# Step sizes of two state-space layers: the bias moved into the product, the correction shared with GpSimd, two PSUM pairs in turn

## What is computed

```python
def _L0_attn_ref(x, A_log, D, W_xproj, W_dt, b_dt):
    x_proj = jnp.einsum('bld,ed->ble', x, W_xproj)
    dtp = x_proj[..., :DT_RANK]                       # 64 columns; 16 of B and 16 of C follow
    dt = jax.nn.softplus(jnp.einsum('blr,dr->bld', dtp, W_dt) + b_dt)
    ...
    # h = exp(dt * A) * h + dt * B * x ;  y = sum over 16 states of h * C ;  y + D * x

def _L1_attn_ref(x, W_delta, W_dt, b_dt, W_B, W_C, A_log, D):
    delta = _softplus_thresh(x @ W_delta @ W_dt + b_dt)     # 128 columns
    ...

x = x + _layernorm(_L0_attn_ref(_layernorm(x), ...))
x = x + _layernorm(_L0_ffn_ref(_layernorm(x), ...))
x = x + _layernorm(_L1_attn_ref(_layernorm(x), ...))
x = x + _layernorm(_L1_ffn_ref(_layernorm(x), ...))
```

## Time and profile before

| | us |
|---|---|
| runs of the kernel before | 656.8, 658.79, 659.71 (median 658.79) |
| span of the profiled execution, first to last instruction | 657.3 |
| granted TensorE clock, mean | 0.977 of full |
| PE / DVE / ACT / POOL busy | 602.7 / 530.2 / 513.7 / 429.1 |
| first stage, to the first scan step | 49.35 |
| scan steps of layer 0 | 49.35 to 206.6 |
| sign product and middle stage | to 282.08 |
| scan steps of layer 1 | 282.08 to 437.6 |
| mixture of experts | to 657.3 |

### The profile page before, as it was taken

How to read it: one execution, slowest core, us unless ns; L and a number is a source line. 1 busy time by engine, 2 the same in 40 slices (tenths; PEclk the granted TensorE clock), 3 DMA queues, 4 the chain that set the end, 5 groups by cost and what they waited for, 6 DMA issues and landing times.

```text
span 657.3 us, 12812 instructions
## 1 busy us (share of the span) xinstructions
PE 602.7 (92%) x4540; PEld 501.7 (76%) x4543; DVE 530.2 (81%) x899; ACT 513.7 (78%) x1182; POOL 429.1 (65%) x261
## 2 busy tenths in 40 slices
PE   5898999999996569799999999999999999999992
PEld 3388999999996434599999999989677555555662
DVE  6798999999998789989999999987863566555374
ACT  2999999999995798899999999967544665444335
POOL 0037999999999302479999999995004277777403
PEclk8979999999999699999999999999999999999997
DMA  7022333333331000044544454438112133333173
GB/s 198 6 67 65 112 112 105 108 109 114 103 110 32 2 0 7 19 147 134 180 128 153 145 159 155 147 91 274 43 64 65 33 97 97 97 99 96 56 265 128
DMA packets 41596, 67.78 MB, mean 103 GB/s; under 512 B 6688, under 2 KB 20928, under 8 KB 41536
## 3 DMA queue, kind: packets, MB, share of 16 engines
q1 hardware_dynamic: 37696, 56.50, 27.5%
q0 software_dynamic: 3840, 10.49, 5.1%
HBM read 57.28 MB, written 9.70 MB: 102 GB/s over the span
## 4 chain that ended last, share of the span: by engine, by line
PE 57%; DVE 14%; ACT 13%; POOL 8%; DMA 4%; issue 3%; DVEq 1%; SPq 0%; ACTq 0%; POOLq 0%
PE both L1383 16%; PE bank L1412 12%; POOL arena L1184 7%; PE both L1476 7%; PE both L1385 5%; PE both L1463 4%; PE bank L1483 4%; DMA arena<-w 2%; ACT rings L1045 2%; PE bank L1404 2%; DVE arena L658 2%; DVE st L443 1%; PE bank L1584 1%; ACT rings L923 1%; ACT tok_a L996 1%
## 5 line engine op out<-in xcount | busy, mean ns | idle before, releaser
L1184 POOL TENSOR_TENSOR arena<-arena,rings 128x1024 f32<-128x1024 f32 x126 | 296.8, 2375 | 17.5 <-DVE arena L658 13.4
L1383 PE MATMUL both<-rings,tok_a 128*128 128x128 f32 x1280 | 183.3, 277 | 3.6 <-DVE arena L658 2.2
L1383 PEld LDWEIGHTS both<-rings,tok_a 128*128 128x128 f32 x1280 | 164.6, 193 | 5.1 <-issue 2.9
L658 DVE TENSOR_TENSOR_SCAN arena<-rings,both 128x1024 f32<-128x1024 f32 x64 | 145.3, 2279 | 12.3 <-PE both L1385 4.5
L658 DVE TENSOR_TENSOR_SCAN arena<-late,both 128x1024 f32<-128x1024 f32 x62 | 140.7, 2278 | 7.1 <-PE both L1385 1.8
L1412 PE MATMUL bank<-ident,arena 128*128 128x128 f32 x1024 | 133.0, 273 | 2.8 <-POOL arena L1184 1.4
L1412 PEld LDWEIGHTS bank<-ident,arena 128*128 128x128 f32 x1024 | 115.7, 141 | 4.2 <-POOL arena L1184 1.9
L1045 ACT ACTIVATE rings<-ident,b_tok 128x128 f32<-128x128 f32 x320 | 106.6, 394 | 0.3
L1045 ACT ACTIVATE rings<-tok_a,b_tok 128x256 f32<-128x256 f32 x192 | 89.7, 500 | 0.0
L1385 PE MATMUL both<-ident,rings 128*128 128x128 f32 x384 | 84.0, 273 | 0.0
L1199 POOL TENSOR_TENSOR arena<-arena,feat_a 128x512 f32<-128x512 f32 x8 | 19.4, 2425 | 86.2 <-DVE arena L554 86.2
(11 more groups left out here) (233 smaller groups left out, 1045.9 us busy)
## 6 DMA issues: line engine op xcount, KB each, us to landing
rings<-c_rows SPq DMA_DIRECT2D x128, 256.0 KB, 3.2
w_sb<-w SPq DMA_DIRECT2D x18, 352.0 KB, 4.2
arena<-w SPq DMA_DIRECT2D x2, 2048.0 KB, 13.2
residual<-x SPq DMA_DIRECT2D x4, 512.0 KB, 5.8
x_rows<-tok_a SPq DMA_DIRECT2D x4, 512.0 KB, 2.6
tok_a<-y_tok SPq DMA_DIRECT2D x4, 512.0 KB, 6.3
w_sb<-y_tok SPq DMA_DIRECT2D x4, 512.0 KB, 7.0
out<-residual SPq DMA_DIRECT2D x8, 256.0 KB, 2.6
```

The lines of the kernel that those rows point to most:

```text
L658: dve.tensor_tensor_scan(h_s, decay_s.rearrange("p h t -> p (h t)"), both[s % B_RING][:, :], 0.0, ALU.mult, ALU.add).then_inc(h_ready, 1)
L1184: pool.tensor_tensor(h_both, h_both, c_row, ALU.mult).then_inc(hc_ready, 1)
L1383: pe.matmul(o, tok_a[:, c, h * P:(h + 1) * P], v_ring[:, s % V_RING, j, 0:P], start=True, stop=True)
```

## The change

It does four things, in both layers:

- **The bias goes into the product.** In layer 0 the tile that holds the projected columns gets a row of ones (row 96; rows 64 to 95 hold B and C), and W_dt gets zero rows and the bias as row 96: one product with 97 rows. In layer 1 all 128 rows are in use, so a second product is added per half (L1306 of the changed kernel): a 128-row block whose first row is the bias, times a 128x512 tile of ones, accumulated in the same bank. The loads of the two bias columns go, one load of a bias block for layer 1 is new.
- **ACT and DVE work is cut.** `Relu` (ACT) and `relu` (DVE) go. `Abs` has no bias. `Exp` and `Ln` take both halves in one instruction of 1024 columns; `Ln` takes 1 + e through its bias and waits for `Exp` only. DVE `near` makes (e + 1) - 1 for both halves in one instruction, and subtracts it from e for half 0; POOL does that for half 1 (`lost`). DVE `dt` then reads the product from PSUM: max(v, 0) + the correction, one instruction per half, and adds the logarithm.
- **PSUM.** `pre` alternates between two pairs of banks, and is released by DVE's `dt` (pre_free) in place of ACT.
- **Order.** The lists are rewritten around this.

```diff
+PRE_ROWS = (64 + 2 * 16 + 1, 128)
...
+        one_row = early[:, 0:SEQ]
+        b_row = early[:, SEQ:SEQ + D]
...
+        pre_pair = [[pairs[1], pairs[2]], [pairs[1], pairs[3]]]
...
-        u_bank = [bank[4:6], bank[6:8]]
+        u_bank = [bank[6:8], bank[4:6]]
...
-            ("x_stat", 0), ("x_norm", 0), ("x_stat", 1), ("x_norm", 1), ("x_stat", 2), ("x_norm", 2), ("x_stat", 3), ("err", 0),
-            ("x_norm", 3), ("ffn", 0), ("err", 1), ("dt", 0), ("err", 2), ("dt", 1), ("b_cols", 1), ("err", 3), ("dt", 2), ("dt", 3)]
+            ("x_stat", 0), ("x_norm", 0), ("x_stat", 1), ("x_norm", 1), ("x_stat", 2), ("x_norm", 2), ("x_stat", 3), ("near", 0),
+            ("x_norm", 3), ("dt", 0), ("ffn", 0), ("near", 1), ("dt", 1), ("near", 2), ("dt", 2), ("b_cols", 1), ("near", 3), ("dt", 3)]
...
-        pool_middle = [("y_add", q) for q in range(Q)] + [("dt", q) for q in range(Q)]
+        pool_first = [("lost", 0), ("dt", 0), ("lost", 1), ("dt", 1), ("lost", 2), ("dt", 2), ("lost", 3), ("dt", 3)]
+        pool_middle = [("y_add", q) for q in range(Q)] + pool_first
...
-                elif name == "err":
-
-                    for h in range(H):
-                        i = k * H + h + 1
-                        dve.wait_ge(exp_ready, i)
-                        dve.tensor_scalar(w_buf[:, h, t], uT[:, h, t], 1.0, None, ALU.add).then_inc(w_ready, 1)
...
+                elif name == "near":
+
+                    if k == Q:
+                        keep()
+                    dve.wait_ge(exp_ready, k + 1)
+                    dve.tensor_scalar(dtT[:, :, t], uT[:, :, t], 1.0, -1.0, ALU.add, ALU.add).then_inc(near_ready, 1)
+                    dve.wait_ge(near_ready, k + 1)
+                    dve.tensor_tensor(dtT[:, 0, t], uT[:, 0, t], dtT[:, 0, t], ALU.subtract).then_inc(lost0_ready, 1)
...
+                        dve.wait_ge(lost_ready if h else lost0_ready, k + 1)
+                        dve.scalar_tensor_tensor(dtT[:, h, t], pre_half(l, q, h), 0.0, dtT[:, h, t], ALU.max, ALU.add)\
+                           .then_inc(head_ready if h == 0 else pre_free, 1)
...
-                        if l == 0:
-                            act.activation(dtT[:, h, t], bank[2 + h][:, :], ACT.Relu, bias=bdt_sb[l][:, h:h + 1])
...
+                    act.wait_ge(exp_ready, k + 1)
+                    act.activation(w_buf[:, :, t], uT[:, :, t], ACT.Ln, bias=ones[:, 0:1]).then_inc(ln_ready, 1)
...
+                    pool.wait_ge(near_ready, k + 1)
+                    pool.tensor_tensor(dtT[:, H - 1, t], uT[:, H - 1, t], dtT[:, H - 1, t], ALU.subtract).then_inc(lost_ready, 1)
...
+                    elif q >= 2:
+                        pe.wait_ge(pre_free, k - 1)
+                    if l:
+                        for h in range(H):
+                            pe.matmul(pre_half(l, q, h), b_row[:, h * P:(h + 1) * P], one_row, start=True, stop=False)
+                    pe.wait_ge(proj_copied, k + 1)
...
+                        if l == 0 and q == 0:
+                            pe.wait_ge(fwT_copied, 1)
+                        stay_busy(turns_behind_u[q], bank[1])
```

More of the change, by code:

```diff
@@ L185, in sandwich_kernel @@
         bank = [both[i // H][:, i % H * SEQ:(i % H + 1) * SEQ] for i in range(H * B_RING)]
-        bank += [ctx.enter_context(nc.psum_tensor(f"bank{i}", [P, 512], F32)) for i in range(H * B_RING, 8)]
+        pairs = both + [ctx.enter_context(nc.psum_tensor(f"pair{i}", [P, H * SEQ], F32)) for i in range(B_RING, 4)]
+        bank += [pairs[i // H][:, i % H * SEQ:(i % H + 1) * SEQ] for i in range(H * B_RING, 8)]
+        pre_pair = [[pairs[1], pairs[2]], [pairs[1], pairs[3]]]
         ysum = bank[4:6]
@@ L274, in sandwich_kernel @@
             ("x_norm", 0), ("r_add", 1), ("r_stat", 2), ("x_stat", 1), ("r_add", 2), ("x_norm", 1), ("r_stat", 3), ("x_stat", 2),
-            ("r_add", 3), ("x_stat", 3), ("x_norm", 2), ("relu", 0), ("x_norm", 3), ("err", 0), ("relu", 1), ("dt", 0), ("err", 1),
-            ("relu", 2), ("dt", 1), ("err", 2), ("relu", 3), ("b_cols", 1), ("dt", 2), ("err", 3), ("dt", 3)]
+            ("r_add", 3), ("x_stat", 3), ("x_norm", 2), ("near", 0), ("x_norm", 3), ("dt", 0), ("near", 1), ("dt", 1), ("near", 2),
+            ("b_cols", 1), ("dt", 2), ("near", 3), ("dt", 3)]
         scalar_middle = [
@@ L574, in stage @@
                     scale(name, q)
-                elif name == "relu":
-                    if k == Q:
-                        keep()
-                    for h in range(H):
-                        dve.wait_ge(pre_used, k * H + h + 1)
-                        dve.tensor_scalar(dtT[:, h, t], bank[2 + h][:, :], bdt_sb[l][:, h:h + 1], 0.0, ALU.add, ALU.max)\
-                           .then_inc(relu_ready, 1)
                 elif name == "r_stat":
@@ L1199, in stage @@
                     pool.tensor_tensor(uT[:, H - 1, t], dtT[:, H - 1, t], feat_a[:, H - 1, t], ALU.mult).then_inc(u_ready, 1)
+            pool.memset(dtpT[PRE_ROWS[0] - 1:PRE_ROWS[0], :], 1.0).then_inc(ones_ready, 1)
+            pool.wait_ge(ones_ready, 1)
+            pool.memset(one_row, 1.0).then_inc(ones_ready, 1)
             for decay in abar_pair:
                 pool.memset(decay[:, :, H - 1, 0:1], 0.0).then_inc(edge_ready, 1)
-            for q in range(Q):
-                stage("dt", q, 0)
+            for name, q in pool_first:
+                stage(name, q, 0)
             product(0)
```

86 lines of the change are left out of this document (37 added, 49 removed).

## The result

| | before | changed |
|---|---|---|
| median of the runs, us | 659.25 (656.8 to 662.13) | 667.01 (664.12 to 669.29) |
| ratio of changed to before | | 1.0108 [1.0074, 1.0142] |
| span of the profiled execution | 657.3 | 664.7 |
| last scan step of layer 0 | 204.25 | 205.83 |
| last scan step of layer 1 | 435.29 | 441.70 |

The change costs 1.1%. (The ratio and its 95% interval are the record's; it is not exactly the quotient of the two medians. The median before is 659.25 with a fourth run, 658.79 with the three that the prediction had.) Of the 7.4 us between the two profiled spans 1.58 arise in layer 0, 4.83 between the two last steps, 1.0 in the experts. The prediction had 0.1, 4.3 and 0.

The account below looks back on a forecast made before the run. PE and DVE were both full in layer 1's middle stage, PE's bias products deciding: span 657.3 + 4.3 (layer 1) + 0.1 (layer 0) = 661.7, plus 1.5 for the runs' median: 663.2 us; range 658.8 to 667.2.

Parts of the forecast that it names:

- Bias pair 1.72, period 8.0, no gap: Layer 1's middle stage on PE: two bias products per quarter cost 1.72 us, period 8.0, last `pre` ends 6.6 later.
- Faster: Rival: DVE sets the middle stage and PE only fills up behind it; total -3 to -5 us, 654 to 656; chance 0.11.
- Nothing to measure: Rival: DVE and POOL follow closely, layer 0 gains 1.2 us, scan catches up; +0.5 to +2.5, 659.3 to 661.3; chance 0.19.
- Much slower: Rival: POOL shut out in both layers, 1.5 to 3 us more in layer 0, 1.5 in layer 1; 666 to 669; chance 0.13.
- PE sets the middle stage: Layer 1, before its scan: PE's added products decide, 6.6 us on PE; last `Exp` at 273.5 against 268.89.
- The chain of dt of quarters 2 and 3 through POOL: Layer 1 entry: DVE waits for POOL until 281.1, dt ready 283.2, so `decays 1` start at 283.5, not ACT's 282.8.
- An entry that ACT sets: Layer 1 scan: 156.1 us from `decays 1` to the last step, as in layer 0, against 157.1 before; +4.3 us in all.
- First stage: Layer 0 up to its scan: ACT's savings of 5 us stay hidden; `decays 1` +0.1 us, from -1.2 to +1.5.
- Reason (a): Layer 0: DVE and POOL work per quarter is 6.2 us against 6.1 before, so no gain.
- Reason (b): Layer 0: the scaling of a_sb, which `decays 0` wait for, moves one quarter later, behind `dt` of quarter 2, to 42.3.
- Exclusion of DVE and POOL: DVE and POOL shut each other out; of a POOL product's 1.65 us about 0.5 is waiting, 1.13 its own.
- The experts "untouched": After layer 1's scan: the experts keep their time and only start later by the same amount; no added cost.

Follow-up runs that it names:

- no_bias1: Changed kernel without the eight bias products of layer 1, whose bias is left out of the result; 658.20 us, ratio to the kernel before 0.9956.
- before_bias: Kernel before, with two bias products (zeros) per quarter of layer 1 added ahead of `pre`; 666.81 us, ratio to the kernel before 1.0108.
- before_load97: Kernel before, with layer 0's W_dt loaded as 97 rows in place of 64; 660.49 us, ratio to the kernel before 1.0006.
- before_again: Kernel before, unaltered, run once more for a second trace; 658.93 us (one run).
- load112: Changed kernel with layer 0's W_dt loaded as 112 rows in place of 97; 665.86 us, ratio to the kernel before 1.0073.
- lost_dve: Changed kernel with the correction of both halves on DVE and none on POOL; 664.34 us, ratio to the kernel before 1.0038.
- mends_lost_dve: Changed kernel with W_dt as 112 rows, layer 1's bias moved from PE to ACT and DVE, both corrections on DVE; 657.09 us, ratio 0.9955.
- early_scale: As mends_lost_dve, but the scaling of a_sb stands behind `near` of quarter 2, not behind its `dt`; 656.23 us, ratio to the kernel before 0.9932.

## Why the prediction was right, and where it was not

- **The total.** The median, 667.01, lies inside the range of 658.8 to 667.2 with 0.2 us to spare, above the forecast's own 661 to 665.5, and 3.8 above 663.2. Direction and main term were right; that the total still fell inside the range is in part luck. As a ratio the forecast was 1.0067 (663.2 / 658.79), and the measurements are 1.0108 [1.0074, 1.0142] and, in twelve more runs, 1.0089 [1.0061, 1.0118]. Of the 3.0 us by which the profiled span exceeds the forecast's 661.7, 1.5 are layer 0, 0.5 the middle stage and 1.0 the tail.
- **Bias pair 1.72, period 8.0, no gap.** All three as the rows show (1.72, 8.01). This term decided: no_bias1 and before_bias put it at 6.8 and 6.15 us, where the prediction had 6.6 on PE.
- **The rivals.** *Faster* (DVE sets the middle stage) falls with before_bias. *Nothing to measure* needed 1.2 us of gain in layer 0, which lost instead. *Much slower* has the measured total in its 666 to 669, but not its mechanism: POOL's product of 4.7 us doesn't occur in the changed kernel, whose longest POOL product there takes 2.25 and whose longest subtraction 1.79.
- **"PE sets the middle stage".** Right for the changed kernel. The last `Exp` came at 276.33; less the 1.58 of layer 0 that is 274.75, where 273.5 was forecast. The 1.25 are the low clock ahead of the first `pre`, a term the sum did not have. In the profiled kernel before, that stretch was at full clock by chance; the other level costs that kernel 0.72 at `decays 1`. The reading of the earlier trace rows, PE without a gap, didn't tell that half a microsecond of it was free.
- **The chain of dt of quarters 2 and 3 through POOL (281.1, 283.2, `decays 1` at 283.5).** Wrong as a mechanism: that dependence doesn't exist. `decays 1` were set by ACT, 9.23 after the last `Exp`. The prediction had ACT's own value, 282.8, and put 0.7 on top (0.3 of it, from 283.2 to 283.5, without a reason); less 1.58 the decays came at 283.98, which is 282.8 + 1.25 within 0.1. An error of 0.7 and a missing 1.25 partly cancel, so +4.3 against a measured 4.83 looks better than its working.
- **An entry that ACT sets takes 156.1 to the last step.** 156.14 here. The figure is right, the reason isn't: from `decays 1` to the last step it is 156.12 to 156.14 in layer 0 of all fourteen profiles and in layer 1 of twelve. The 157.1 of the kernel before (and 157.10 in before_load97) isn't another kind of entry, but the low clock at its first scan steps. So the 1.0 us that the prediction subtracted is a clock level in one profile and not a gain of the change. Against before_again, without that loss, "between" is 5.07 longer in the changed kernel.
- **First stage +0.1.** Measured 1.58, just past the bound of 1.5 that the prediction had named for being wrong, and itself a sum of three things. The late x is 2.06 (load112, at like clock). The rest of the change is 0.87: load112 against before_again, both with full clock between 12 and 16 us and 0.50 between 36 and 40 (203.77 against 202.90). And 1.35 goes off, because the first profile of the kernel before had lost that much against before_again, with its clock at 0.57 between 12 and 16. The 0.87 goes with PE: the fourth `pre` starts 0.3 earlier in load112 (32.29 against 32.59), but behind the wait of 3.91, and it takes 3.78 in place of 2.38. Reason (a), no gain on DVE and POOL, fits. Reason (b) has the place of the scaling right (42.31), but in the changed kernel the late turned u set `decays 0`; the wait of 2.75 for the scaling shows in lost_dve and mends_lost_dve, where PE kept its clock. What failed is the conclusion that the loads cost nothing, from "end long before the first `pre`" and "SP issues one load less": both may hold, but what a load's shape does to the loads of x behind it was not asked. And no term stood for PE's wait of 3.91 for the freed bank and the clock that fell behind it.
- **Exclusion of DVE and POOL.** 1.13 of its own per POOL subtraction, as read from the earlier trace rows. By the Trainium skill (SBUF — State Buffer, "Who interferes with whom") one holder keeps the other out for one whole instruction. The trace agrees here: POOL's row at 21.89 is 0.64 of waiting for DVE's subtraction (ends 22.53) and 1.13 of its own, and DVE's copy ends with it. It does not in the two POOL products of 4.7 us in the earlier trace rows, which several DVE instructions passed. The price was in small instructions (0.16 to 1.24) that the count of big ones left out.
- **The experts "untouched".** Their tail runs from 221.0 to 226.4 in fourteen profiles, in step with the granted clock between 40 and 60 us behind the last scan step: 221.0 to 222.0 where that is 1.00, 222.6 to 223.4 at 0.91, 225.3 at 0.83, 226.1 and 226.4 at 0.74. The kernel before had 1.00 and the changed kernel 0.91, which accounts for the +1.0.

## What to carry to other kernels

Ask which engine will be the bound once the work is moved, and put work on it last: two additions hidden in existing DVE instructions per quarter did for 0.2 us what eight products on a full PE did for 6.8. A load's shape is a cost of its own: here 112 rows in place of 97 freed the queue behind it, so look at the issues behind a load and not only at its end. Compare two profiles stretch by stretch at the same granted clock before a difference of 1 or 2 us is explained. And before a chain is summed over several engines, read from the wait's own arithmetic which data it stands for.

## What was not expected of the hardware

- One level of PE's clock costs the changed kernel 1.25 us ahead of the first `pre` of layer 1, and up to 2.2 at 12 to 18 us (the fourth `pre` at 30.62 in mends_lost_dve and at 32.86 in early_scale, with the same queue and loads). The kernel before lost 0.96 to it at its first scan steps, and the tails, with no edit in them, differ by 5.4. Profiles of one kernel differ mostly in these places.
- PE was at the lower clock (0.50 to 0.53 between 36 and 40 us) in all six profiles in which it had waited 3.9 us before the fourth `pre`, in one of four with a wait of 2.3, and in all four of the kernel before's kind, with waits of 1.8 to 2.0 and shorter ones ahead. What decides it was not found.
- A VectorE copy of four columns takes 0.16 or 1.24 us, by whether a GpSimd subtraction is running.
